# A table of scaled rows is written to memory from POOL's queue instead of SP's

## The reference

```
x = _layernorm(x + L0(x, edges))     # two graph convolutions, 128 -> 256 -> 128
x = _layernorm(x + L1(x, edges))     # attention messages, a GRU cell, a batch norm

# one graph convolution of L0
h = x @ W
deg = segment_sum(ones, dst) + 1.0
dinv = rsqrt(deg)
msg = h[src] * (dinv[src] * dinv[dst])[:, None]
agg = segment_sum(msg, dst) + h * (dinv * dinv)[:, None]
out = agg + b
```

## Time and profile before

| | |
|---|---|
| median of 3 runs | 2106.43 us |
| profiled execution | 2114.78 us, of which the span of the instructions is 2113.0 us |
| mean granted TensorE clock in it | 0.932 |
| busy share of the span | PE 77%, DVE 66%, ACT 58%, POOL 44% |
| queue of SP (q1) | 342.01 MB, 47.4% of the 16 DMA engines |
| queue of POOL (q0) | 39.34 MB, 8.8% of them |
| scaling stage | about 98 to 218 us |

### The profile page before, as it was taken

How to read it: one execution, slowest core, us unless ns; L and a number is a source line. 1 busy time by engine, 2 the same in 40 slices (tenths; PEclk the granted TensorE clock), 3 DMA queues, 4 the chain that set the end, 5 groups by cost and what they waited for, 6 DMA issues and landing times.

```text
span 2113.0 us, 37476 instructions
## 1 busy us (share of the span) xinstructions
PE 1635.4 (77%) x8258; PEld 1096.5 (52%) x8258; DVE 1393.5 (66%) x4915; ACT 1220.3 (58%) x3127; POOL 934.6 (44%) x911
## 2 busy tenths in 40 slices
PE   7600577777777777568888889969999999995664
PEld 2100355555555555356666667635555555554553
DVE  8926355555555555356666666548888888887897
ACT  0186344444444444246666666647777777775788
POOL 2000544444544444266666666266666666630000
PEclk8955799999999999879999999989999999997898
DMA  7397444443333333247776665557777444428987
GB/s 234 112 332 284 134 141 144 141 142 110 101 102 103 101 103 99 98 148 251 247 260 222 195 196 189 189 176 228 228 228 211 131 126 126 129 84 306 358 282 248
DMA packets 218927, 382.39 MB, mean 181 GB/s; under 512 B 38959, under 2 KB 41228, under 8 KB 218832
## 3 DMA queue, kind: packets, MB, share of 16 engines
q1 hardware_dynamic: 190272, 342.01, 47.4%
q0 software_dynamic: 28560, 39.34, 8.8%
HBM read 222.75 MB, written 177.81 MB: 190 GB/s over the span
## 4 chain that ended last, share of the span: by engine, by line
PE 65%; DVE 10%; issue 9%; ACT 6%; DMA 6%; ACTq 1%; another core or an unknown queue 1%; DVEq 1%; SPq 1%; POOL 0%; POOLq 0%
PE bank L1330 10%; PE bank L1293 9%; PE bank L1314 8%; PE bank L1380 4%; PE bank L1306 4%; PE bank L1366 4%; PE bank L1368 4%; PE bank L1370 4%; PE bank L1372 4%; PE bank L1373 4%; ACT page L735 3%; PE bank L1349 3%; DVE onehot L1081 2%; PE bank L1352 2%; DVE gath L1204 2%
## 5 line engine op out<-in xcount | busy, mean ns | idle before, releaser
L668 POOL DMA_INDIRECT gath<-XP,ROWI x294 | 302.0, 1027 | 511.4 <-PE bank L1306 255.7
L668 POOL DMA_INDIRECT gath<-MT,ROWI x294 | 325.1, 1106 | 206.7 <-PE bank L1380 107.6
L668 POOL DMA_INDIRECT gath<-G,ROWI x294 | 294.7, 1003 | 207.5 <-PE bank L1330 101.7
L735 ACT ACTIVATE page<-bank,b_sb 128x512 f32<-128x512 f32 x196 | 124.1, 684 | 361.1 <-PE bank L1314 352.5
L1041 DVE TENSOR_SCALAR onehot<-iota_b,LOC,WD 128x170 f32<-128x170 f32 (+1 forms) x294 | 108.4, 422 | 316.0 <-PE bank L1306 298.8
L1293 PE MATMUL bank<-w_sb,page 128*128 128x128 f32 x1568 | 202.7, 283 | 145.7 <-ACT page L735 140.3
L1293 PEld LDWEIGHTS bank<-w_sb,page 128*128 128x128 f32 x1568 | 184.0, 193 | 226.7 <-ACT page L735 173.7
L1330 PE MATMUL bank<-gath,onehot 128*128 128x128 f32 x1176 | 164.5, 292 | 76.8 <-DVE onehot L1081 34.0
L1330 PEld LDWEIGHTS bank<-gath,onehot 128*128 128x128 f32 x1176 | 146.3, 200 | 84.5 <-issue 66.0
L1314 PE MATMUL bank<-page,w_sb 128*128 128x512 f32 x392 | 184.4, 593 | 0.0
L1400 PE MATMUL bank<-ident,page 128*128 128x128 f32 x784 | 126.8, 310 | 72.8 <-DMA page<-YT 67.6
(11 more groups left out here) (215 smaller groups left out, 3572.5 us busy)
## 6 DMA issues: line engine op xcount, KB each, us to landing
page<-YT SPq DMA_DIRECT2D x196, 256.0 KB, 4.1
MT<-page SPq DMA_DIRECT2D x98, 260.0 KB
XP<-page SPq DMA_DIRECT2D x98, 256.0 KB, 2.1
G<-page SPq DMA_DIRECT2D x98, 256.0 KB
OWN<-page SPq DMA_DIRECT2D x98, 256.0 KB
page<-OWN SPq DMA_DIRECT2D x98, 256.0 KB
YT<-page SPq DMA_DIRECT2D x98, 256.0 KB
page<-AD SPq DMA_DIRECT2D x98, 256.0 KB
```

What stands on the lines that cost most here:

```text
L668: nc.gpsimd.indirect_dma_start(gath[k][:, w, 0:width], None, rows, bass.IndirectOffsetOnAxis(ap=ROWI[:, at:at + 1], axis=0), bounds_check= ...
L735: last = nc.scalar.activation(rows[k], bank[2 + 2 * k + h][:], ACT.Relu, bias=b1_sb[:, h:h + 1])
```

## The change

The write and its waits leave SP's step and become a step of POOL's own, ahead of POOL's wait for all writes. SP's pass has a lag of 0 then, since only the reads are left in it, and POOL's has a lag of 0 too: at each step it waits for the group's scaling and begins the write.

```
             def scale(group_of):
                 if (g := group_of(0)) and not g.kept:
                     k = g.slot(4)
                     wait(sp, s_done, g.freed(4))
                     sp.dma_start(s_x[k], group_of_table(x, g)).then_inc(x_in[k], 16)
-                if g := group_of(3):
-                    k = g.slot(4)
-                    done, half = in_register(sp, g.done()), in_register(sp, g.done() - FREE)
-                    wait(sp, s_done, done)
-                    if g.kept:
-                        wait(sp, s_half, half)
-                    sp.dma_start(group_of_table(XP, g), s_o[k]).then_inc(s_st[k], 16)
-
-            run_pass(sp, scale, 3)
+
+            run_pass(sp, scale, 0)
             wait_all_dmas(sp, s_st)
...
+            def scale(group_of):
+                if g := group_of(0):
+                    k = g.slot(4)
+                    done, half = in_register(pool, g.done()), in_register(pool, g.done() - FREE)
+                    wait(pool, s_done, done)
+                    if g.kept:
+                        wait(pool, s_half, half)
+                    nc.gpsimd.dma_start(group_of_table(XP, g), s_o[k]).then_inc(s_st[k], 16)
+
+            run_pass(pool, scale, 0)
             pool.wait_ge(ready, 1)
             wait_all_dmas(pool, s_st)
```

## The result

The changed kernel takes 2119.03 us (median of 4 runs, 2116.66 to 2120.95) against 2105.64 us before (4 runs). The ratio is 1.0062, with a 95% interval of 1.0045 to 1.008: 9.5 to 17 us slower. Run again beside other experiments it gave 1.004 (1.0022 to 1.0058). Both intervals hold 9.5 to 12 us. The forecast was +26.6 us, 2133.0: right in direction, about twice too large.

The account below looks back on a forecast made before the run. It took a loop of reads and scaling to bound the first half, VectorE near its limit the second, and POOL's 1.30 us step the second afterwards: 0 + 26.0 + 0.66 = +26.6 on 2106.43, 2133.0 us, range 2112 to 2156.

Parts of the forecast that it names:

- The first half's 0: Scaling of the 44 groups not kept (98 to 167 us): POOL's step and the output buffers fit, cost 0, ends -5 and +10.
- The buffers' way: First half: an output buffer's round of scaling, hand-over, POOL's DMA and landing takes 5.8 us for four groups, under 6.10.
- the reads' loop: First half: read of x, ScalarE's scaling, write issue and next read issue on SP take 6.10 us per four groups.
- POOL's instruction: Each write DMA moved to POOL takes 1.00 us like its indirect gathers; with a 0.30 us gap, 1.30 us a step.
- The bound from below: Lowest time for a plain DMA on POOL: SP's issue of the same transfer, 0.34 us, or 0.64 with POOL's gap.
- The failed step: Second half (kept groups, 176 to 216 us): POOL's 1.30 us a step replaces 0.791 over 51 steps, +26.0 us.
- the right quantity: Second half: a buffer's own loop with POOL's DMA is 3.8 us, 0.96 a group, said not to decide.
- The end: End of the scaling stage: the last write lands 1.00 + 1.69 us after POOL starts it instead of 2.03, +0.66 us.
- The middling POOL: Rival, 12 in 100: POOL takes 0.9 to 1.0 us a step in the second half; +8.8 us, 2115.2 us.
- The exclusion of VectorE and POOL: Rival, 12 in 100: the two take turns in the second half, 1.98 us a step; +61.3 us, 2167.7 us.
- The first rival: 8 in 100: POOL's plain DMA is short and SP's freed queue speeds the first half; -4.3 us, 2102.1 us.
- the fourth: Rival, 13 in 100: the first half slows too, by longer landings, +10 us on top of the forecast, 2143.0 us.

## Why the prediction was right in direction, and wrong in mechanism and size

- **The stretch and the place.** Right. The loss lies in the kept half; the split of the stage between POOL and SP showed it, with a first half that costs nothing in the stage. The first half's 0 came out, for one of the two reasons given. POOL's step fits. The buffers' way does not stay inside the reads' loop: I had put it at 5.8 us, with SP's hand-over of 0.16 us; with the measured 0.64 and a landing of 4.1 us from the start it is 1.28 + 0.64 + 4.1 = 6.0 us, and some 0.2 more until ScalarE begins on the buffer again, against the loop's 6.10. So ScalarE waited 11 times for a write to land. The reads did gain, ScalarE's waits for them fell from 7.0 to 3.1 us, and the 4.8 us of waits for landings took it back. That the two balance was not foreseen.
- **POOL's instruction.** The mis-sized term. I took 1.00 us from the gathers and got 0.539. That their time didn't follow their rows (0.99 us for 98, 1.00 for 128) I read as a fixed cost of any DMA on POOL; among the gathers of the rows read that holds, and a plain DMA takes about half of theirs. Also, POOL stands 0.19 us between two plain ones, not the gathers' 0.30. The bound from below (0.34) was closer than the value taken (0.46 us away against 0.20).
- **What decides in the second half.** The failed step: "POOL issues one write after the other, and a step of 1.30 us is longer than 0.791". POOL's own step proved to be 0.73 us when buffers were plenty, below 0.791. The prediction worked out the right quantity one line further, "3.8 us, 0.96 a group, which is not what decides". It was 3.91 and 0.978, and it decided. That 3.8 was so close is luck: two terms in it were off and cancelled. POOL's instruction was 0.46 us shorter than assumed, and the hand-over, which I had left as it was on SP, was 0.71 instead of 0.23 us. The direction too came out by a path other than the one forecast.
- **The end.** The last write landed 2.4 us after its start instead of 2.0 (first gather 5.0 us after the write began, 4.6 before): +0.4 where I had +0.66.
- **The sum** with what was measured is 51 x 0.187 + 0.4 = +9.9 us, inside both intervals of the time. The forecast had +26.6.
- **The rivals.** The middling POOL (+8.8 us, 12 in 100) had the right size, by a pace that was not the limit. The exclusion of VectorE and POOL is ruled out here: POOL's writes take a median of 0.539 us in the changed kernel, in both halves, and a mean of 0.55 us in the eight-buffer kernel with VectorE busy 26.48 of 30 us, where they start 0.19 us after one another; VectorE's multiplications take a mean of 0.283 us beside them and 0.282 before. The exclusion was the rule of the Trainium skill, "SBUF — State Buffer", section "Who interferes with whom"; its lock, if it was taken, shows in no duration of these runs. The first rival (SP's freed queue makes it faster) failed: a POOL step under 0.79 us, its condition, was there with eight buffers, though with an instruction above 0.49 us, and the gain was not. Of the fourth, a slower first half, the rows show at most 0.9 us (44 writes in 68.4 instead of 67.5 us; 67.7 when the changed kernel was run again).
- **What would have told it.** The waits of before named it: ScalarE and VectorE waited for landings 21 and 17 times at a step of 0.791, above VectorE's 0.68. The second half was a loop through four buffers already then, and every 0.1 us put on the way of a buffer costs 0.025 us a step. I priced the new engine's throughput, and what the four buffers pay for is its latency.

## What to carry to other kernels

Where a few buffers go round between an engine and the DMA queue, take the round's time (work, hand-over, instruction, landing) and divide it by the number of buffers; that, and not the queue's pace, is the step as long as the waits for landings are many. In this kernel, moving the writes to a queue that starts them later cost the extra latency once for each round, and more buffers bought it back: eight buffers took the writes on POOL to within 0.2% of the kernel before, and gave the kernel before itself 0.3%. Don't take one kind of DMA as the price of another on the same engine.

## What the runs showed of the hardware

- A plain DMA of 128 rows x 2 KB keeps POOL busy 0.539 us, an indirect one of 128 rows 1.00 us. Back to back in a loop POOL begins a plain one every 0.73 us.
- POOL begins a DMA 0.29 us after the engine that it waits for is done when the instruction is written out with one wait, 0.54 us with two; in a loop with values from registers it is 0.64 us with one and 0.71 with two. SP in a loop takes 0.16 us with one and 0.23 with two. All are medians.
- Writes from SBUF with nothing beside them ran at 327 GB/s with four buffers; with eight they ran at 381 GB/s from SP and at 336 GB/s from POOL.
